# ScalarE's high part of the attended values between the two swap copies of a head, in a two-layer attention and expert kernel

## What is computed

```python
Q = _apply_rope(Q, cos, sin); K = _apply_rope(K, cos, sin)      # 16 heads of 128
scores = jnp.einsum('bhqd,bhkd->bhqk', Q, K) / math.sqrt(DH)
attn = jax.nn.softmax(scores + mask[None, None], axis=-1)       # 64 keys back at most
out = jnp.einsum('bhqk,bhkd->bhqd', attn, V)
out = _lora_proj(out, wo, oA, oB, lora_scale)
return residual + out
```

## Time and profile before

| what | value |
|---|---|
| median of 3 executions | 1182.82 us (1181.33 to 1185.87) |
| profiled execution, its own time | 1184.07 us |
| profiled execution, span of the trace | 1182.2 us |
| granted TensorE clock, mean | 0.961 of full speed |
| TensorE matmul busy | 1010.5 us, 85% |
| VectorE busy | 849.3 us, 72% |
| ScalarE busy | 673.5 us, 57% |
| GpSimd busy | 604.3 us, 51% |

### The profile page before, as it was taken

The page is one execution under the profiler, slowest core; times in us unless marked ns, Lnnn a source line. Parts: engine busy times, 40 slices in busy tenths (PEclk is TensorE's granted clock), DMA queues, the critical chain, the costliest instruction groups (busy, mean ns, idle before and its releaser), DMA issues.

```text
span 1182.2 us, 21240 instructions
## 1 busy us (share of the span) xinstructions
PE 1010.5 (85%) x6229; PEld 677.7 (57%) x6229; DVE 849.3 (72%) x2233; ACT 673.5 (57%) x1720; POOL 604.3 (51%) x596
## 2 busy tenths in 40 slices
PE   4966798845788899899999999999978889999984
PEld 2544543323456576567666766666664568886442
DVE  4586566845587768867668888888874787776677
ACT  1532344514657765876966556656664777775332
POOL 0468465512666567554544555554542145552774
PEclk9988999977999999999999999999998999999997
DMA  9777599977454257041110011210016745554443
GB/s 342 297 202 283 96 330 301 298 257 224 76 131 99 94 113 159 13 96 38 50 59 4 34 36 37 85 37 1 1 61 212 202 119 146 145 142 101 134 123 101
DMA packets 96956, 156.00 MB, mean 132 GB/s; under 512 B 12208, under 2 KB 67248, under 8 KB 94032
## 3 DMA queue, kind: packets, MB, share of 16 engines
q1 hardware_dynamic: 77120, 115.48, 29.8%
q0 software_dynamic: 19728, 39.21, 14.9%
HBM read 104.91 MB, written 45.02 MB: 127 GB/s over the span
## 4 chain that ended last, share of the span: by engine, by line
PE 38%; DVE 18%; ACT 17%; issue 10%; DMA 5%; DVEq 4%; POOL 3%; ACTq 2%; POOLq 1%; SPq 1%
PE ps L1234 5%; ACT arena L1482 5%; PE ps L1068 4%; ACT arena L1459 3%; PE ps L1180 3%; DMA arena<-in_wdn 3%; PE ps L883 3%; PE ps L1128 2%; PE ps L1197 2%; DVE arena L2001 2%; ACT arena L1458 2%; PE ps L1081 2%; ACT arena L1475 2%; PE ps L1252 2%; PE ps L1097 2%
## 5 line engine op out<-in xcount | busy, mean ns | idle before, releaser
L2287 POOL TENSOR_TENSOR arena<-arena 128x512 f32<-128x512 f32 x128 | 160.4, 1270 | 144.3 <-ACT arena L1459 143.5
L1068 PE MATMUL ps<-arena 128*128 128x512 f16 x768 | 178.5, 382 | 19.5 <-ACT arena L1459 19.5
L2294 POOL TENSOR_TENSOR arena<-arena 64x512 f32<-64x512 f32 x128 | 137.1, 1071 | 113.2 <-DVE arena L1946 109.5
L1458 ACT ACTIVATE arena<-ps 64x512 f32<-64x512 f32 x128 | 76.0, 594 | 154.3 <-DVE arena L1918 150.2
L1068 PEld LDWEIGHTS ps<-arena 128*128 128x128 f16 x768 | 73.0, 98 | 119.3 <-ACT arena L1459 32.7
L2332 POOL DMA_INDIRECT wvo<-xn_d,idx x79 | 75.9, 960 | 113.6 <-PE ps L1224 96.9
L1482 ACT ACTIVATE arena<-arena 128x192 f32<-128x192 f32 x256 | 112.5, 444 | 2.4 <-DVEq L1941 2.4
L1081 PE MATMUL ps<-wvo,arena 128*128 128x512 f16 x384 | 94.6, 383 | 12.2 <-issue 5.9
L1097 PE MATMUL ps<-arena 128*128 128x192 f32 x512 | 96.7, 332 | 7.2 <-DVE arena L1924 5.4
L1128 PE MATMUL ps<-wvo,arena 128*128 128x256 f16 x768 | 96.4, 278 | 1.8 <-DVE arena L1958 1.4
L1924 DVE TENSOR_TENSOR arena<-arena 128x512 f32<-128x512 f32 x128 | 88.2, 729 | 7.9 <-POOL arena L2287 7.9
(11 more groups left out here) (293 smaller groups left out, 2166.1 us busy)
## 6 DMA issues: line engine op xcount, KB each, us to landing
arena<-wqk_d SPq DMA_DIRECT2D x16, 1024.0 KB, 5.2
arena<-in_wgu SPq DMA_DIRECT2D x32, 384.0 KB, 11.0
y_d<-wvo SPq DMA_DIRECT2D x79, 128.0 KB, 2.4
z_d<-wvo SPq DMA_DIRECT2D x8, 1024.0 KB, 4.2
z_d<-wvo SPq DMA_DIRECT2D x2, 4096.0 KB, 27.8
arena<-in_wdn SPq DMA_DIRECT2D x32, 192.0 KB, 14.2
arena<-z_d SPq DMA_DIRECT2D x12, 512.0 KB, 4.4
arena<-z_d POOLq DMA_DIRECT2D x12, 512.0 KB, 7.3
```

The costliest lines, as they stand in the source:

```text
L1068: last = pe.matmul(ps[s][:, :], wqk[gg][:, s * DC + c, w, hh * DH:(hh + 1) * DH], hx[bb][:, :, x, c * P:(c + 1) * P], start=(c == 0 and w ...
L1458: nc.scalar.activation(qk_s[0:64, s], ps[s][64:P, :], ACT.Copy)
L2287: nc.gpsimd.tensor_tensor(qk_s[:, s], qk_s[:, s], sin, ALU.mult).then_inc(sin_done, 1)
L2294: nc.gpsimd.tensor_tensor(pm[u][rows, at:at + SEQ].rearrange("p (t n) -> p t n", t=TPB), pp[u][rows, :, at:at + P], ri[rows].unsqueeze(2). ...
```

## The change

In ScalarE's loop over the passes, `output_high(h - 1)` stands between `swap(h + 2, 0)` (with `turned_rows`, where there is one) and `swap(h + 2, 1)`, where it stood behind both. In the last two passes there is no swap, and nothing changes there.

```diff
@@ -1505,10 +1505,10 @@
                     shared_high(1)
                 for t in tiles_at(FOLLOW_AT, h - 1):
                     turned_rows(t, 2)
+                if h:
+                    output_high(h - 1)
                 if h + 2 < NH:
                     swap(h + 2, 1)
-                if h:
-                    output_high(h - 1)
                 if h + 1 < NH:
                     exponentials(h + 1, (h + 1) % 2)
                 probs_out(h)
```

## The result

The changed kernel took **1205.64 us** (median of 4 executions, 1204.44 to 1206.34) against 1184.34 for the kernel before beside it (4 executions, 1181.33 to 1187.52): ratio 1.0171, 95% interval 1.0134 to 1.0208. The forecast was 1196.1 with a range up to 1201. The direction was right, the size was not, and the range was too narrow. Of the 9.5 us between 1205.6 and 1196.1, 1.5 are the base (the forecast started from 1182.82) and 8.0 are the change's cost (21.3 against 13.3).

The account below looks back on a forecast made before the run. No single engine was taken to bound the kernel; the stage alternates between TensorE stretches and a chain through ScalarE, VectorE and GpSimd. Terms 2.0 + 6.6 + 4.1 + 0.6 = 13.3 us gave 1196.1 us, range 1187 to 1201.

Parts of the forecast that it names:

- the passes without an output sum: Passes finishing an earlier tile: later reciprocal delays GpSimd's normalisation; 20 passes at 0.1 us, 2.0 us (0 to 4).
- the first end of a stretch: First TensorE-only stretch, passes 9 to 14: second rotary sum, already held by GpSimd, starts 0.46 us later.
- exponentials: ScalarE: same three instructions stand ahead, so where the attention product is early they begin unchanged, 0 us.
- ends of TensorE stretches: Swap 1 waits behind the late attention product, paid only at stretch ends: three at 1.22, one 0.46, 4.1 us.
- passes with an output sum: Even passes from 6: rotary sum collides with GpSimd's second sine; 11 at 0.55, three at 0.2, 6.6 us.
- from the first cosine of pass 61 on: Last pass with swaps: swap 1 waits for the late attention product, 0.6 us (0 to 1.2).
- the rival in which it becomes the bound: TensorE's projection slips beyond its 0.52 us idle time; 4 us on top, 1200 us; 11%.
- The lock between a VectorE instruction with two SBUF inputs and a GpSimd product: The two exclude each other for a whole instruction, first one winning; without it the sum is 6 us less.
- the rival in which the one-hot work slips ahead: VectorE keeps its turn for all four one-hots, saving 0.84 us in 16 passes; 1182.7 us, not slower; 7%.
- The rival by which only the ends of stretches count: VectorE's and GpSimd's new order is free as probabilities-out still waits for L1464; 4.1 us, 1186.9 us; 12%.

Follow-up runs that it names:

- second pair: Also called the repetitions: the kernel before, unchanged, and the changed kernel, run again on one chip; changed kernel 1235.49 us, ratio 1.0141.
- r_steady: Changed kernel with the old order kept in passes 10 to 14, 21 to 24, 29 to 34, 37 and 38: 1227.36 us, ratio 1.0094.

## Why the prediction was right or wrong

The direction was right, and the mechanism in the main. These steps of the prediction failed: the code that the edit doesn't touch was put at nothing, in the sum and in the range, where it gave 5.0 us in the profiled pair; the passes without an output sum were taken at 2.0 us and cost 3.6; the first end of a stretch was taken at 0.46 and cost 1.36; and the exponentials were said to begin when they did, where they begin 0.13 later. With the base of 1184.34 and the 15.6 us of the edited part alone the time would have been 1199.9, within the range.

Change minus before, from the first cosines in the first pair of profiles (us):

```
part                                          forecast   measured
4 ends of TensorE stretches                   4.1        5.4  (1.36 1.32 1.39 1.35)
17 other passes with an output sum            6.6        5.9  (8 table passes 3.16)
25 passes without one, or hardly touched      2.0        3.6
from the first cosine of pass 61 on           0.6        0.6
passes 0 and 1                                0          1.1  (-0.33 in the second pair)
code that the edit doesn't touch              0          5.0  (5.30 ahead, -0.25 behind)
```

**The mechanism was right**, in the order of its steps, here for pass 54: swap 1 0.6 later, the low part's wait gone, the second sine product beginning at +3.83, the rotary sum inside it held until 0.5 behind its end (832.15, from 830.43 + 1.72, against 831.61), the reciprocal 0.58 later. TensorE kept idle time within the projection (0.37 ahead of its second half at 830.31), so the rival in which it becomes the bound didn't come about. In pass 61 swap 1 waited for the high part as forecast, and the exponentials began 4.41 behind the cosine instead of 3.65, 0.76 where 0.6 was taken. That the whole time behind it also grew by 0.63 is luck, given 27.32 and 30.74 in the repetitions.

The lock between a VectorE instruction with two SBUF inputs and a GpSimd product, for which the prediction cited the Trainium skill (SBUF — State Buffer, "Who interferes with whom"), is now shown by an experiment: 1.72 us in pass 54 of the changed kernel, 0.69 with the output sum out of its way. The kernel before had it in more places than the one that the prediction read: the first rotary sums at 302.48 and 313.33 take 1.81 and 1.74 us beside a sine product.

**Exponentials: put at no change, and 0.13 later.** The prediction reasoned that the same three instructions stand ahead of them. But the last of the three is now a swap copy, and the engine's rows show another distance behind it than behind the high part. Timeline, kernel before, passes 34 and 53:

```profile
627.00 1.36 PE L1116 MATMUL ps<-arena 128*128 128x192 f32 x8
...
628.89 0.45 ACT L1482 ACTIVATE arena<-arena 128x192 f32<-128x192 f32 x1
...
801.73 0.45 ACT L1482 ACTIVATE arena<-arena 128x192 f32<-128x192 f32 x1
```

The first exponential begins 0.49 behind the start of the high part (801.24 in pass 53), and 0.61 behind that of the last swap copy in the changed kernel (829.67 to 830.28 in pass 54). From the cosine it is 3.64 before and 3.77 after, and L1464 moves from 5.65 to 5.79. Why the two copies differ isn't shown. These 0.13 are about what the other ends of stretches cost above 1.22 (below), and L1464's 0.14 is about what the passes pay that end on probabilities-out.

**Ends of stretches: the term for the first end was mis-sized**, 0.46 where 1.36 was measured. I let the start of GpSimd's sine in pass 14 stand at 443.34 and moved only swap 1 within that pass. That start isn't fixed. Before, a DMA that GpSimd issues (L2302) stood ahead of it:

```profile
441.63 1.64 POOL L2302 DMA_DIRECT2D arena<-z_d  x1
...
443.34 2.50 POOL L2287 TENSOR_TENSOR arena<-arena 128x512 f32<-128x512 f32 x2
```

and after, with the attention product that this pass waits for:

```profile
450.09 1.36 PE L1116 MATMUL ps<-arena 128*128 128x192 f32 x8
...
450.91 1.65 POOL L2302 DMA_DIRECT2D arena<-z_d  x1
...
452.63 2.49 POOL L2287 TENSOR_TENSOR arena<-arena 128x512 f32<-128x512 f32 x2
```

The sine is 3.91 behind the cosine in both (cosines at 439.43 and 448.72), but the cosine stands 2.74 ahead of the attention product before (442.17) and 1.37 after. The other engines had lost 1.37 against TensorE in the passes before, hidden, and pass 14 is where that falls due. Pass 34 is the same case. Timeline, changed kernel, beside the earlier trace rows:

```profile
639.51 1.36 PE L1116 MATMUL ps<-arena 128*128 128x192 f32 x8
...
640.90 0.60 ACT L1475 ACTIVATE arena<-ps 128x512 f16<-128x512 f32 x1 [0.87 <-PE ps L1116]
...
642.13 0.59 ACT L1459 ACTIVATE arena<-ps 64x512 f32<-64x512 f32 x1
...
642.75 0.46 ACT L1482 ACTIVATE arena<-arena 128x192 f32<-128x192 f32 x1
```

The exponentials begin 3.24 behind the product, 1.89 before (628.89 and 627.00): 1.35, which is the 1.22 taken and the 0.13 above. Inside the stretch nothing is lost: from the attention product of pass 33 to that of 34 it is 8.13 us in both kernels (618.87 to 627.00; 631.38 to 639.51). Counted by cosines the loss shows at the start of a stretch (pass 10 +1.02, 21 +1.37, 29 +1.24), because the other engines lose their lead over TensorE there; the attention products come later only behind the stretch.

**Passes without an output sum: mis-sized.** I took 0.1 in 20 of them and counted those that end on L1464 as free. The reciprocal moved by 0.18 instead of the 0.13 worked out, and the passes that end on the normalisation passed it on: 0.15 to 0.18 each in 2, 3, 4, 15, 17, 19 and the odd table passes. To take 0.1 instead of the 0.13 was a choice, and the run with the later reciprocal shows that it had no ground. And the passes that end on L1464 weren't free, since L1464 itself came 0.14 later: pass 9 paid 0.14. And the row has 25 passes, where the forecast counted 20.

**Passes with an output sum: right in sum, by two errors.** The reciprocal is 0.58 later, as worked out, but a table pass is only 0.42 longer. Because the reciprocal no longer precedes L1464, probabilities-out follows it at once (832.76), the one-hots start 0.42 behind the normalisation instead of 0.82, and one more of them is done within it (0.65, 0.29, 1.02 and 0.29 us against 0.29, 1.14, 0.29 and 0.29 in pass 55; the long one ends with GpSimd's second product): L2003 follows the normalisation's end by 0.17 (835.28 against 835.11) and in odd passes by 0.38 (844.39 against 844.01). That is a part of the rival in which the one-hot work slips ahead, at 0.2 a pass and not 0.84. The four passes 8, 18, 40 and 42 cost the full 0.57 to 0.59, though 40 had been taken at 0.2; 16, 26, 36 and 60 cost between -0.13 and 0.16, and 28 cost 0.28. That 60 pays 0.16 and not 0.58 is L1464's lateness: in the run with the output sum moved its reciprocal is 0.41 earlier and the pass is as long.

**The range was too narrow** for a reason that isn't in the kernel's order at all. It was made of the bounds of the terms only. Runs of the same code differ in how long TensorE is granted only the lower clock ahead of the attention and behind it, and in how long those stages take. The three ratios measured for this change, 1.0171, 1.0141 and 1.0118, have intervals that share 1.0134 to 1.015; the middle of it is some 17 us, of which the traces place 14.9 to 15.2 in passes 2 to 60. The first figure of 21.3 holds some 5 us from ahead of the attention, as far as its one profiled pair tells. What starts or ends the lower clock in those stages wasn't tried, so it stays open.

Without that the forecast was 13.3 against 15.6 from pass 2 to the end of the stage: 0.9 more for the first end, 0.4 for the other three, 1.6 for the passes without an output sum, and 0.7 less for those with one.

The rival by which only the ends of stretches count is refuted by r_steady (+9.9 with the stretches left as they were).

## What to carry to other kernels

Before a copy is put between two feeders of another engine, look at who waits behind the *second* feeder: here the copy's own reader stopped waiting (48.1 to 9.5 us) and the feeder's reader began to (7.9 to 61.6). A loss that a saturated engine hides is kept and falls due in full at the end of the stretch, so price it once per stretch by the other engines' distance to it, not by the local order of the last pass. And give a range the spread of untouched code between executions as well as the bounds of the terms.

## What was not expected of the hardware

The same code ahead of the attention ended anywhere from 307.49 to 319.26 us (first cosine of pass 0) in 13 profiles, with a granted clock of 0.79 to 0.87 from 150 to 307 us, while passes 2 to 60 of one kernel repeated to 0.4 us at a granted clock of 1.00. From the first cosine of pass 61 to the end it took 315 to 319 us in six profiles and 339 to 342 in the seven taken on chips 14 and 3, so a time from one chip isn't to be held against one from another.

Four one-hot instructions took 1.77 or 2.02 us beside the same normalisation, and the longer time came with the shorter way from the reciprocal to the next cosine (3.21 us in pass 54, 3.36 in pass 55 of the changed kernel): it is how many of them get in before each of GpSimd's products that counts. Pass 54 with the output sum moved shows it alone: with the same reciprocal and normalisation as in pass 55 (5.76 and 6.01 behind the cosine) two of them, and not one, are done ahead of the second product, and the pass takes 8.99 instead of 9.12.
